# Output projection folded into the stored values; the FFN part turns the attention output with PE transposes

## The reference, cut to what matters

```python
q = hidden_states @ Wq.T + bq
scores = einsum('bshd,hmd->bshm', q, memory_keys) / sqrt(128)
probs = softmax(scores)
mem_out = einsum('bshm,hmd->bshd', probs, memory_values)
attn = mem_out @ Wo.T + bo
x = layernorm(x + attn)
h = silu((x @ w1.T) * s1) * ((x @ w2.T) * s2)
h = gelu((h @ h1.T) * h1_s)
h = gelu((h @ h2.T) * h2_s)
x = layernorm(x + (h @ w3.T) * s3)
```

## Time and profile before

| What | Value |
|---|---|
| median of 3 runs | 1205.12 us (1204.24 to 1205.73) |
| the profiled execution | 1209.24 us |
| its span, first to last instruction | 1207.4 us |
| mean granted clock of PE in it | 0.972 |
| busy: PE, PEld, DVE, ACT, POOL | 1126.3, 919.2, 976.5, 899.4, 734.1 us |
| DMA moved | 162.96 MB |
| v load, each of 4: 512 KB | 12.2 us to landing |
| key load, each of 4: 512 KB | 6.4 us to landing |

### The profile page before, as it was taken

The page is one execution under the profiler, slowest core; times in us unless marked ns, Lnnn a source line. Parts: engine busy times, 40 slices in busy tenths (PEclk is TensorE's granted clock), DMA queues, the critical chain, the costliest instruction groups (busy, mean ns, idle before and its releaser), DMA issues. The chain is left out here.

```text
span 1207.4 us, 20221 instructions
## 1 busy us (share of the span) xinstructions
PE 1126.3 (93%) x5376; PEld 919.2 (76%) x5376; DVE 976.5 (81%) x1774; ACT 899.4 (74%) x1579; POOL 734.1 (61%) x608
## 2 busy tenths in 40 slices
PE   4699999999999999999999999745999999999996
PEld 2488788888888888888888887424788888888885
DVE  3888888889888888888888888265678888888875
ACT  4577788878778778778787877613888888888883
POOL 3288889889889889888888888862012112112110
PEclk8899999999999999999999999976999999999998
DMA  7778888888888888888888888811000101101000
GB/s 150 176 164 196 193 189 194 199 189 193 199 188 193 198 189 196 198 191 191 198 193 189 198 187 188 221 31 55 18 27 27 52 26 30 48 26 36 25 10 27
DMA packets 85506, 162.96 MB, mean 135 GB/s; under 512 B 19296, under 2 KB 48864, under 8 KB 85472
## 3 DMA queue, kind: packets, MB, share of 16 engines
q1 hardware_dynamic: 85472, 162.55, 57.3%
HBM read 19.87 MB, written 8.39 MB: 23 GB/s over the span
## 5 line engine op out<-in xcount | busy, mean ns | idle before, releaser
L251 POOL TENSOR_TENSOR pT<-slot_p,pT 128x512 fp32r<-128x512 f32 x512 | 653.8, 1316 | 116.3 <-ACT pT L290 116.3
L424 PE MATMUL o_ps<-pT,v_hi 128*128 128x512 f32 x1024 | 393.0, 406 | 23.1 <-POOL pT L251 22.7
L362 DVE TENSOR_SCALAR_CACHE_REDUCE rows<-s_ps 128x1024 f32<-128x1024 f32 x256 | 313.2, 1224 | 83.4 <-PE s_ps L410 70.3
L290 ACT ACTIVATE pT<-slot_p 128x512 fp32r<-128x512 f32 x512 | 297.7, 619 | 100.6 <-DMA slot_p<-rows 65.0
L331 DVE STREAM_TRANSPOSE rows<-rows 128x1024 f32<-128x1024 f32 x256 | 317.2, 1240 | 2.7 <-ACT rows L281 2.7
L281 ACT ACTIVATE rows<-rows,bias 128x1024 f32<-128x1024 f32 x256 | 292.2, 1142 | 16.2 <-DVE bias L368 14.4
L426 PE MATMUL o_ps<-pT,v_lo 128*128 128x256 f32 x1024 | 288.9, 282 | 0.0
L424 PEld LDWEIGHTS o_ps<-pT,v_hi 128*128 128x128 f32 x1024 | 195.0, 190 | 91.2 <-POOL pT L251 46.1
L408 PE MATMUL s_ps<-keys,q_buf 128*128 128x512 f32 x512 | 210.9, 412 | 21.6 <-DVE rows L362 16.2
L426 PEld LDWEIGHTS o_ps<-pT,v_lo 128*128 128x128 f32 x1024 | 195.8, 191 | 18.9
L802 PE MATMUL ring<-h_hi,keys 128*128 128x512 f32 x512 | 203.6, 398 | 1.7 <-DVE h_lo L705 1.5
(11 more groups left out here) (76 smaller groups left out, 1102.1 us busy)
## 6 DMA issues: line engine op xcount, KB each, us to landing
slot_p<-rows SPq DMA_DIRECT2D x1024, 128.0 KB, 2.3
x_in<-in_xT SPq DMA_DIRECT2D x32, 128.0 KB, 2.1
o_scratch<-o_sum SPq DMA_DIRECT2D x32, 128.0 KB, 1.9
o_in<-o_scratch SPq DMA_DIRECT2D x16, 256.0 KB, 2.9
x_in<-in_x SPq DMA_DIRECT2D x16, 256.0 KB, 3.2
out<-y_out SPq DMA_DIRECT2D x16, 256.0 KB, 2.3
slot_p<-in_kT SPq DMA_DIRECT2D x4, 512.0 KB, 6.4
slot_p<-in_v SPq DMA_DIRECT2D x4, 512.0 KB, 12.2
```

Source lines behind the costliest of these rows:

```text
L251: nc.gpsimd.tensor_tensor(halves(s % RING, 1), slots_first(pp, s), halves(s % RING, 0).bitcast(FP32), ALU.subtract).then_inc(split, 1)
L290: nc.scalar.activation(halves(s % RING, 0), slots_first(pp, s), ACT.Copy).then_inc(highed, 1)
L362: nc.vector.tensor_scalar(row_piece(tile, k), s_ps[:, j % 2, :], 1.0, None, ALU.mult, ALU.max, accum_out=part_max[:, tile, k:k + 1]).then_ ...
L424: nc.tensor.matmul(o_ps[:, pp, :], v_hi[:, 2 * s + c, :], pT[:, s % RING, c, :], start=first, stop=False, skip_group_check=True)
```

## The change

Since probs @ V @ Wo.T is the same as probs @ (V @ Wo.T), the new kernel forms V @ Wo.T once, in frame 0 of the attention part. The values now come transposed and permuted on the host (`in_vT`, four pieces with rows of 4 KB, features on partitions). In steps t = 8 to 15 of frame 0 PE multiplies a half piece (512 slots) by Wo: four fp32 matmuls of 128x128 into one of the two banks of `o_ps`. ACT copies each half piece out of PSUM twice: rounded, to v_hi, and in full, to the place of the raw keys (once all keys are split). POOL subtracts by halves (eight subtractions in place of four). In the FFN part the load and split of Wo and the split of o go, and PE turns o_in by four fp32 transposes against the identity.

```diff
@@ sync, start
             load_x(1)
-            for g in range(GROUPS):
-                sp.dma_start(v_raw[g * G:(g + 1) * G, :].rearrange("r (c d) -> r c d", d=P),
-                             v[g, :, :, :]).then_inc(v_loaded[g], 16)
+            sp.dma_start(wo[:, :], woT).then_inc(wo_loaded, 16)
+            for n in range(PIECES):
+                sp.dma_start(piece(v_in, n), piece(vT, n)).then_inc(v_loaded[n], 16)
@@ gpsimd, start
-            for n in range(PIECES):
+            for n in range(HALVES):
                 pool.wait_ge(v_high, n + 1)
-                nc.gpsimd.tensor_tensor(piece(v_lo_flat, n), piece(v_raw, n), piece(v_hi_flat, n).bitcast(FP32),
+                pool.wait_ge(v_copied, n + 1)
+                nc.gpsimd.tensor_tensor(half_piece(v_lo_flat, n), half_piece(v_raw, n), half_piece(v_hi_flat, n).bitcast(FP32),
                                         ALU.subtract).then_inc(v_split, 1)
@@ scalar, frame
-                    if is_step(f, 0) and t in (4, 5, 6, 7):
-                        n = t - 4
-                        for g in range(GROUPS):
-                            act.wait_ge(v_loaded[g], 16)
-                        nc.scalar.activation(piece(v_hi_flat, n), piece(v_raw, n), ACT.Copy).then_inc(v_high, 1)
+                    if is_step(f, 0) and t >= STEPS - HALVES:
+                        n = t - (STEPS - HALVES)
+                        act.wait_ge(v_made, n + 1)
+                        nc.scalar.activation(half_piece(v_hi_flat, n), o_ps[:, n % 2, :], ACT.Copy).then_inc(v_high, 1)
+                        if n == 0:
+                            for part in range(PIECES):
+                                act.wait_ge(k_split[part], 1)
+                        nc.scalar.activation(half_piece(v_raw, n), o_ps[:, n % 2, :], ACT.Copy).then_inc(v_copied, 1)
@@ tensor, frame, behind the scores of step t
+                    if is_step(f, 0) and t >= STEPS - HALVES:
+                        n = t - (STEPS - HALVES)
+                        if n == 0:
+                            pe.wait_ge(wo_loaded, 16)
+                        if n % 2 == 0:
+                            pe.wait_ge(v_loaded[n // 2], 16)
+                        at_least(pe, v_copied, n - 1)
+                        for c in range(HALF // P):
+                            at = n * HALF + c * P
+                            last = nc.tensor.matmul(o_ps[:, n % 2, c * P:(c + 1) * P], v_in[:, at:at + P], wo[:, :],
+                                                    start=True, stop=True, skip_group_check=True)
+                        last.then_inc(v_made, 1)
@@ ffn, sync
-                    sp.wait_ge(o_split, i + 3)
+                    sp.wait_ge(y_done, i + 3)
@@ ffn, scalar
-            act.wait_ge(wo_loaded, 16)
-            nc.scalar.activation(wo_hi[:, :], wo_raw[:, :], ACT.Copy).then_inc(wo_high, 1)
...
-                if valid(i + 3, BLOCKS):
-                    o_high_part(i + 3, i2 + 1 + par, 1 - par)
@@ ffn, vector
-            dve.wait_ge(wo_high, 1)
-            nc.vector.tensor_tensor(wo_lo[:, :], wo_raw[:, :], wo_hi[:, :].bitcast(FP32), ALU.subtract).then_inc(wo_split, 1)
...
-                if valid(i + 3, BLOCKS):
-                    o_low_part(i + 3, 1 - par)
@@ ffn, tensor
-                for b in rows_blocks(i):
-                    pe.wait_ge(o_split, b + 1)
+                for n, b in enumerate(rows_blocks(i)):
+                    o_par = n if filling(i) else par
+                    pe.wait_ge(o_loaded[o_par], 16 if filling(i) else 16 * i2 + 32)
                     at_least(pe, z1_ready, 4 * b)
-                    wh, wl = wo_hi[:, :], wo_lo[:, :]
                     for s in range(4):
-                        oh, ol = o_hi[:, s * P:(s + 1) * P], o_lo[:, s * P:(s + 1) * P]
-                        nc.tensor.matmul(y_ps[:, s, :], oh, wh, start=True, stop=False)
-                        nc.tensor.matmul(y_ps[:, s, :], oh, wl, start=False, stop=False)
-                        last = nc.tensor.matmul(y_ps[:, s, :], ol, wh, start=False, stop=True)
+                        last = nc.tensor.transpose(y_ps[:, s, :], o_in[:, o_par, s * P:(s + 1) * P], ident[:, :])
                     last.then_inc(y_done, 1)
```

More of the change, by code:

```diff
@@ L39 @@
 PIECES = SLOTS // PIECE
+HALF = PIECE // 2
+HALVES = SLOTS // HALF
 T_LAG = 14
@@ L73, in valid, with attention @@
     return not isinstance(index, int) or 0 <= index < end
-def attention(nc, xT, wqT, bq, kT, v, weights, o_dram, o_stored, den, keys, rows, low_max):
+def attention(nc, xT, wqT, bq, kT, vT, woT, weights, o_dram, o_stored, den, keys, rows, low_max):
     ctx = ExitStack()
@@ L113, in attention @@
         k_loaded = [sem(f"k_loaded{n}") for n in range(PIECES)]
-        v_loaded = [sem(f"v_loaded{g}") for g in range(GROUPS)]
-        wq_loaded, bq_loaded, w_loaded = map(sem, ("wq_loaded", "bq_loaded", "w_loaded"))
+        v_loaded = [sem(f"v_loaded{n}") for n in range(PIECES)]
+        wq_loaded, wo_loaded, bq_loaded, w_loaded = map(sem, ("wq_loaded", "wo_loaded", "bq_loaded", "w_loaded"))
         x_loaded, q_projected, q_high, q_split = map(sem, ("x_loaded", "q_projected", "q_high", "q_split"))
-        k_high, v_high, v_split = map(sem, ("k_high", "v_high", "v_split"))
+        k_high, v_made, v_high, v_copied, v_split = map(sem, ("k_high", "v_made", "v_high", "v_copied", "v_split"))
         k_split = [sem(f"k_split{n}") for n in range(PIECES)]
@@ L129, in attention, with half_piece @@
         v_lo_flat = v_lo[:, :, :].rearrange("p c d -> p (c d)")
+        def half_piece(t, n):
+            return t[:, n * HALF:(n + 1) * HALF]
         def piece(t, n):
@@ L205, in exchange @@
                     if is_step(p, 1):
-                        sp.wait_ge(v_split, PIECES)
+                        sp.wait_ge(v_split, HALVES)
                         for n in range(PIECES):
@@ L420, in frame @@
                             if is_step(p, 0):
-                                pe.wait_ge(v_split, PIECES)
+                                pe.wait_ge(v_split, HALVES)
                         for c in range(2):
@@ L431, in _, with ffn @@
             frames(pe, frame)
-def ffn(nc, x_rows, woT, bo, scale_cols, o_dram, o_stored, den, keys, rows, low_max, out_rows):
+def ffn(nc, x_rows, bo, scale_cols, o_dram, o_stored, den, keys, rows, low_max, out_rows):
     ctx = ExitStack()
@@ L461, in ffn @@
         xb = sb("xb", [P, 4, P], FP32)
-        o_hi = sb("o_hi", [P, BT], FP32R)
-        o_lo = sb("o_lo", [P, BT], FP32R)
         z1 = sb("z1", [P, 4, P], FP32)
@@ L610, in load_table @@
                 nc.scalar.activation(table_spare[:, 0:1], minus_half[:, 0:1], func).then_inc(table_loaded, 1)
-            def o_high_part(b, b2, par):
-                act.wait_ge(o_loaded[par], 16 * b2 + 16)
-                at_least(act, y_done, b)
-                nc.scalar.activation(o_hi[:, :], o_in[:, par, :], ACT.Copy).then_inc(o_high, 1)
             def gates(b):
@@ L682, in _ @@
             dve.wait_ge(rden_ready, 2)
-            def o_low_part(b, par):
-                dve.wait_ge(o_high, b + 1)
-                nc.vector.tensor_tensor(o_lo[:, :], o_in[:, par, :], o_hi[:, :].bitcast(FP32), ALU.subtract).then_inc(o_split, 1)
             def products(b):
@@ L898, in program @@
         weights = {"w1": t["w1T"], "w2": t["w2T"], "h1": t["h1T"], "h2": t["h2T"], "w3": t["w3T"]}
-        attention(nc, t["xT"], t["wqT"], t["bq"], t["kT"], t["v"].rearrange("(g c r) d -> g r c d", g=GROUPS, r=G), weights,
+        attention(nc, t["xT"], t["wqT"], t["bq"], t["kT"], t["vT"], t["woT"], weights,
                   o_dram, o_stored, den, keys, rows, low_max)
         tiled = "(t p) d -> p t d"
-        ffn(nc, t["x"].rearrange(tiled, p=P), t["woT"], t["bo"], (t["s1"], t["s2"], t["s_h1"], t["s_h2"], t["s3"]),
+        ffn(nc, t["x"].rearrange(tiled, p=P), t["bo"], (t["s1"], t["s2"], t["s_h1"], t["s_h2"], t["s3"]),
             o_dram, o_stored, den, keys, rows, low_max, out.rearrange(tiled, p=P))
@@ L915 @@
         "bq": lay(a["L0_attn_bq"].reshape(P, 1)), "bo": lay(a["L0_attn_bo"]),
-        "kT": lay(a["L0_attn_memory_keys"][0].T), "v": lay(a["L0_attn_memory_values"][0]),
+        "kT": lay(a["L0_attn_memory_keys"][0].T), "vT": lay(v.transpose(3, 1, 0, 2).reshape(P, SLOTS)),
         "w1T": lay(a["L0_ffn_w1_w"].T), "w2T": lay(a["L0_ffn_w2_w"].T), "h1T": lay(a["L0_ffn_h1_w"].T),
```

19 lines of the change are left out of this document (7 added, 12 removed).

## The result

The changed kernel takes **1189.35 us** (median, 1188.72 to 1189.45) against 1205.26 (1204.24 to 1205.73) for the kernel before beside it: ratio 0.9868, 95% interval 0.9851 to 0.9885, so 15.9 us less, where 16.1 had been forecast. On another occasion the same two gave 1188.68 against 1206.70, ratio 0.9852 (0.9836 to 0.9867), so 18 us less. The profiled execution after took 1189.26 us, span 1187.5; the one before had lain 4 us above its median, so the two profiles differ by more (19.9 us) than the timings do.

The account below looks back on a forecast made before the run. PE was taken to bound steady attention and FFN, ACT's wait for v and its copies the start; 5.0 us (start) plus 11.1 (FFN) off 1205.12 gave 1189.0 us, range 1184.5 to 1197.

Parts of the forecast that it names:

- FFN, 11.1 forecast: All FFN turns plus the fill: 10 x 0.67 + 3 x 0.8 + 0.4 + 1.6 = 11.1 us off, bounds 7 to 15.
- PE's gain and the gate: FFN loop turn: PE freed of 0.94 us, but ACT's third Silu gate holds h2, so 0.67 us gained.
- The turns outside the loop: FFN turns 1, 12 and 13: 0.8 us gained in each.
- x norm: FFN turn: ready 0.18 us before PE needs it, no stall; rival that it stalls PE, 1191.4 us, chance 0.09.
- Transposes: FFN turn: four take 0.35 us for 12 matmuls' 1.29; rival, full duration, 1.2 us for four, 1196.8, chance 0.02.
- Fill: Start of the FFN part: xb becomes z's releaser, 1.3 us, plus var_eps 0.36; 1.6 us, between 0.9 and 3.0.
- Start, 5.0 forecast: Frame 0 of attention: ACT no longer waits for v, third transpose near 31.5 against 36.65, 5.0 us off.
- The whole chain moves with it: Start: SP's unbroken sends and ACT's first high part move with the third piece's transpose, 5.1 us, taken as 5.0.
- The dear fold: Frame 0 rival: a fold matmul costs 0.43 us, not 0.22; start 1 us worse than before, 1195 us, chance 0.15.
- the start has another holder: Rival: the start gains nothing and only the FFN gains, 1194 us, chance 0.04.
- the gate chain moves along: FFN rival: full 0.94 us each turn, or entry sooner with up to 1.4 of the fill, 1184.5 us, chance 0.08.
- the slower case: Frame 0 rival: PE waits for ACT's copies and drops to the lower clock, about 1210 us, chance 0.04.

Follow-up runs that it names:

- start_only: New attention part with the kernel before's FFN part, so the output projection is applied twice: 1203.0 us, ratio 0.9960 to the kernel before.
- ffn_only: Kernel before's attention part with the new FFN part, so the output projection is left out: 1197.02 us, ratio 0.9912 to the kernel before.
- turned_twice: Changed kernel with the four transposes of the attention output made twice in each turn: 1191.96 us, ratio 0.9875 to the kernel before.
- low_kept: Changed kernel with a DVE subtraction of two idle tiles where o_lo had been: 1190.78 us, ratio 0.9867 to the kernel before.
- before_again: The kernel before, unchanged, timed and profiled once more: 1207.77 us, ratio 1.0002.
- after: The changed kernel itself in its first profile: median 1189.35 us, ratio 0.9868 to the kernel before.
- fold_later: Changed kernel with the fold and its copies moved from frame 0 to frame 1, t = 0 to 7: 1185.95 us, ratio 0.9831 to the kernel before.
- after_again: The changed kernel, unchanged, timed again on another occasion: 1188.68 us, ratio 0.9852 to the kernel before.
- copies_late: Kernel before with ACT's four copies of v moved from t = 4 to 7 to t = 12 to 15 of frame 0: 1197.67 us, ratio 0.9916.

## Why the prediction was right, and where it was not

The time, 1189.35 against 1189.0, is right, but by a closer fit than its terms deserve, and in part by luck: the second occasion gave 18 us instead of 16.

**FFN, 11.1 forecast.** By the table the new part takes 384.4 to 386.4 us against 396.1 to 396.6, which is 9.7 to 12.2 (start_only with its pause, and the two kernels with added work in it, left aside); by timing `ffn_only` gives 10.6.
- *PE's gain and the gate.* 0.94 freed, 0.67 kept: the turn is shorter by 22.45 - 21.79 = 0.66, and h2 starts 6.58 us after w3, as worked out. `turned_twice` shows the free time. What the prediction left out is that most of it, 0.18 us, is spent before h2, where PE waits for DVE's first product, a link of the same chain; the wait at the gate itself is 0.05 and not the 0.2 that it named as a sign. The fourth gate came sooner (the pair takes 1.25 in place of 1.48), the third did not.
- *The turns outside the loop.* 0.8 forecast; turns 1 and 13 went from 22.48 and 22.44 to 21.62 and 21.54, so by 0.86 and 0.90.
- *x norm.* No stall, right. The slack was 0.42 rather than 0.18, and `low_kept` shows that a kept o_lo would have eaten it without a real stall; this rival was further off than the 0.09 says.
- *Transposes.* 0.36 for four, at a clock of 0.99. The prediction worked out 0.33 us for a single one and said that the trace disagrees with the page. Both need putting right. The group of z2T transposes in the kernel before has this row (shortest, median and longest duration in ns):

```profile
L850 PE MATMUL z_ps<-ident,z2T x64: 270/272/329, 879.2 to 1200.2; 128*128 128x128 f32 x64
```

  So one takes 0.272 us, and the four start 0.11 apart and overlap (0.11 is also what each added one cost in `turned_twice`, 0.44/4). The Trainium skill (TensorE: Matmul & The Clock Gate, Part 4: PE-mode transpose) gives about 275 ns for one, and the trace agrees. What the trace contradicts is only the prediction's own step of adding four durations to 1.1 us. Whether transposes count for the clock, no run here can show, since dense matmuls stand around them.
- *Fill.* xb did become the releaser. z comes 1.75 us sooner relative to the part's first issue, 0.39 of it because the issue of wo's load is gone from the front of SP's queue; var_eps adds 0.36. 1.6 had been given for both. PE's entry, costed at nothing, did come sooner too (its idle time there is 12.72 us against 14.8 to 15.4 in the profiles of the old part), but z waits for xb and gets nothing of it.

**Start, 5.0 forecast: the term that was mis-sized.** Up to the third transpose the working holds: 0.20 us a fold matmul (0.22), a step of 1.59 us (1.58), PE and ACT about even, third transpose 31.1 to 32.0 (31.5). The step that failed is "The whole chain moves with it": the prediction tied the first high part to the third transpose, from which it read the run of sends. The sends run on from the first transpose, and that one moved by 6.2 us (means of the table: 30.8 to 24.7) where the third moved by 5.2. The high part moved by 6.8 (56.4 to 49.6), and the attention part by 8.1 (810.6 to 802.4), where 5.0 had been forecast. Of the last 1.3 us, some is probably the clock: in the 8 us from the first products with v on, the granted clock was 0.59 before and 0.79 after, as these windows (before, then after) show; the rest wasn't tried apart.

```profile
56.00:64.00 8.00, 5.81 (x16) 4.75 (x17) 5.13 (x9) 7.84 (x14) 6.75 (x6) 0.59 0.88 206
```

```profile
50.00:58.00 8.00, 5.72 (x22) 4.69 (x22) 5.18 (x9) 7.74 (x14) 6.64 (x6) 0.79 0.87 206
```

**Why the sum came out all the same.** By the profiles the two parts gain 8.1 and about 11.3 us, 19.4 in all; the timings say 15.9 and 18. Less the 10.6 of `ffn_only`, that leaves about 5 and 7 for the start. The two profiled executions of the kernel before took 1209.2 and 1207.5 us, above most of its medians (1205.3 to 1207.4 over the four occasions), so these two profiles overstate the difference by one or two us. Part of the scatter is the clock after the fill, which the reader can see in the stretch between the x transposes of turns -1 and 0: 26.1 to 26.6 us where the granted clock is 1.00 in it (before_again, after, turned_twice, fold_later), 28.2 to 28.5 where it is 0.94 (ffn_only, start_only, low_kept, after_again). The changed kernel is on both lists, so this differs from execution to execution. The intervals of the two timings have 16 to 18 us in common, with the forecast at the lower edge; what is missing up to the upper edge is the start's.

**The rivals.** The dear fold is excluded by 0.20 us a matmul; that the start has another holder, or that the change does nothing, by `start_only`; that the gate chain moves along, by the turn of 21.79, which would be 21.51; the slower case by a step of 1.59 us at full clock.

## What to carry to other kernels

When a wait moves, look for the first link of the chain that then runs without a break (here the first piece on a DMA queue), not for the last one before the stretch that you can read easily. An engine that waits for a load early in a hand-written order holds all that stands behind it: here a move by eight steps gave 10 us, with no change to the computation. Folding a matrix into a constant operand is cheap (here 6.5 us of PE), but do it where the engines wait anyway, and not ahead of the first piece of the pipeline; and before crediting a DMA with a wait because a chain names it, move the DMA and look.

## What the runs showed that I had not expected

- The same 2 MB moved at 175 to 193 GB/s as rows of 512 bytes (32 partitions to a DMA) and at 340 to 420 as rows of 4 KB (128 partitions to a DMA), into the same buffer; the prediction had left the pace of the new load open.
- The whole gain of the start, and more, lies in an order of instructions that was open to the kernel before (`copies_late`, 1197.67).
- A tiny addition on GpSimd (128x4) takes 0.20 us alone and 0.56 beside a DVE subtraction of two SBUF tiles; `low_kept` brings this back with idle tiles, so it is contention and not a dependency. The addition ends 0.06 us after the subtraction does, in both kernels (919.31 against 919.25 in `low_kept`).
- PE can stop for 2.25 us in a row of twelve matmuls with no releaser (`start_only`), and the entry of the FFN part costs PE 12.6 to 13.4 us of "issue" idle time in every version with the new FFN, 14.8 to 15.4 with the old one.
